# The first layer of a two-layer transformer kernel: from a looped order of phases to an unrolled pipeline of 20 slots a batch

## The reference

```python
# self attention: rows quantised to 8 bit, ternary weights, 16 heads of 16
q, k, v = bitlinear(x, w_q), bitlinear(x, w_k), bitlinear(x, w_v)
attn = softmax(causal(q @ k.T / sqrt(16)))
x = layernorm(x + bitlinear(attn @ v, w_o))
# cross attention: channels are the 128 rows, 16 heads of 8, 256 positions, rope, a mask
q, k, v = wq @ x + bq, wk @ ctx + bk, wv @ ctx + bv
scores = where(mask == 0, -1e4, rope(q).T @ rope(k) / sqrt(8))
x = layernorm(x + wo @ (softmax(scores) @ v) + bo)
```

## Time and profile before

| | us |
|---|---|
| median of 3 runs (lowest, highest) | 1825.73 (1823.53, 1825.94) |
| the profiled execution | 1822.41 |
| its span | 1820.6 |
| PE busy | 1453.8 (80%) |
| DVE busy | 999.8 (55%) |
| ACT busy | 609.2 (33%) |
| POOL busy | 366.7 (20%) |

### The profile page before, as it was taken

One profiled execution on the slowest core, in us unless ns is written; L12 is line 12 of the kernel. 1 busy time (PEld: TensorE's weight loads), 2 busy tenths in 40 slices (PEclk: granted clock), 3 DMA queues, 4 the chain that ended last, 5 costly groups with the idle time before them and its releaser, 6 DMA issues. The chain is left out here.

```text
span 1820.6 us, 29862 instructions
## 1 busy us (share of the span) xinstructions
PE 1453.8 (80%) x9331; PEld 863.5 (47%) x9331; DVE 999.8 (55%) x2735; ACT 609.2 (33%) x1389; POOL 366.7 (20%) x507
## 2 busy tenths in 40 slices
PE   2478888878888787539999996558888886799997
PEld 1234444444444443226566564335565553466664
DVE  5256666666666665242222222357887763467775
ACT  0133333334333332212232232225566543233231
POOL 1211112112111110011111111445555430000000
PEclk9589999999999998769999998678999998799999
DMA  4323222222223221054111111384455420200000
GB/s 127 104 47 51 47 45 50 48 48 50 53 52 53 47 40 22 29 193 133 36 35 31 34 33 36 76 186 98 115 116 120 104 64 19 74 1 12 12 1 24
DMA packets 165279, 112.22 MB, mean 62 GB/s; under 512 B 32682, under 2 KB 155818, under 8 KB 165040
## 3 DMA queue, kind: packets, MB, share of 16 engines
q1 hardware_dynamic: 150256, 95.09, 23.1%
q0 software_dynamic: 3408, 9.31, 2.0%
q10 hardware_dynamic: 11504, 6.46, 1.3%
HBM read 46.48 MB, written 12.45 MB: 32 GB/s over the span
## 5 line engine op out<-in xcount | busy, mean ns | idle before, releaser
L910 ACT ACTIVATE first_probs<-pair 128x512 f32<-128x512 f32 x320 | 177.6, 595 | 131.3 <-PE pair L411 129.0
L452 DVE TENSOR_REDUCE first_negmax_x<-bank 128x2 f32<-128x512 f32 x256 | 169.0, 685 | 64.0 <-PE bank L396 57.7
L396 PE MATMUL bank<-kept_stack_cross 96*128 96x256 bf16 x768 | 156.1, 286 | 11.4 <-DMA kept_stack_cross<-second_parts_x_q 9.5
L1891 ACT ACTIVATE second_probs<-pair 128x512 f32<-128x512 f32 x192 | 113.7, 598 | 130.7 <-PE pair L411 115.5
L411 PE MATMUL pair<-kept_stack_cross 98*128 98x256 bf16 x768 | 151.3, 280 | 1.5 <-DMA kept_stack_cross<-second_rows_x 1.0
L389 PE MATMUL bank<-kept_mask_q,kept_ident 128*128 128x512 bf16 x256 | 104.8, 409 | 57.4 <-DMA kept_stack_cross<-first_parts_x_q 31.6
L1405 PE MATMUL pair<-kept_w,experts_hidden_t 128*128 x312 | 140.3, 592 | 0.0
L452 DVE TENSOR_REDUCE second_negmax_x<-bank 128x2 f32<-128x512 f32 x128 | 88.6, 692 | 60.4 <-PE bank L396 52.5
L396 PEld LDWEIGHTS bank<-kept_stack_cross 96*128 96x128 bf16 x768 | 75.7, 103 | 75.5 <-issue 26.2
L404 PE MATMUL pair<-kept_mask_t,kept_ident 128*128 128x512 bf16 x256 | 100.8, 394 | 11.7 <-ACT first_probs L910 8.3
L1446 ACT ACTIVATE experts_hidden_t<-bank,kept_b 128x128 f32<-128x128 f32 x156 | 44.6, 368 | 183.2 <-PE bank L1380 183.2
(11 more groups left out here) (430 smaller groups left out, 2965.7 us busy)
## 6 DMA issues: line engine op xcount, KB each, us to landing
kept_stack_self<-first_parts_a SPq DMA_DIRECT2D x128, 64.0 KB, 3.1
kept_w<-in_L_ffn_W SPq DMA_DIRECT2D x8, 1024.0 KB, 7.1
kept_stack_self<-second_parts_a SPq DMA_DIRECT2D x128, 64.0 KB, 3.4
kept_stack_cross<-first_parts_x_k SPq DMA_DIRECT2D x96, 64.0 KB
kept_stack_cross<-first_parts_x_q SPq DMA_DIRECT2D x96, 64.0 KB
kept_stack_cross<-second_parts_x_k SPq DMA_DIRECT2D x96, 64.0 KB, 2.5
kept_stack_cross<-second_parts_x_q SPq DMA_DIRECT2D x96, 64.0 KB
expert_out<-experts_expert_done SPq DMA_DIRECT2D x39, 128.0 KB, 1.8
```

Of the source, the lines that this page charges most:

```text
L396: mm = pe.matmul(out, q, k, start=mask is None, stop=True, skip_group_check=True)
L452: return dve.tensor_reduce(negmax[:, 2 * n:2 * n + 2], bank[:, :].rearrange("p (m t) -> p m t", t=D), AX.X, ALU.max, negate=True)
L910: act.activation(probs[(phase + n) % PROBS][:, :], key_bank[n % KEYBANKS][:, :], ACT.Exp, scale=att.scale).then_inc(probs_made, 1)
L1891: act.activation(probs[i % PROBS][:, :], key_bank[i % 2][:, :], ACT.Exp, scale=att.scale).then_inc(probs_made, 1)
```

## The change

run_steps, Counts and step are gone. In their place stands the table of the second layer with 20 slots a batch: each step has an offset, and step f of batch b is done in slot 20 b + f. Each engine goes through all slots and does in each what falls in it, in a fixed order: first the slot's score bank and key bank. Own scores lie at 0 to 3, cross scores at 39 and 44 to 58, own keys at 9 to 12, cross keys at 65 to 68 and 73 to 84, so every slot of a full lap has one score bank and one key bank, of different batches: when batch b has its own scores, b-2 has its cross scores and b-3 or b-4 its cross keys. Buffers are added for it: three of x0, kv, the cross stack, four of x1, twelve probs tiles in place of eight. DVE has a drain at the end of each slot.

The small matmuls get other banks: `work` for what is made of rows and context, `small_bank` for turned maxima, sums, y and logits. The lay of the reciprocals is issued by ACT, no more by SP. DVE's own_heads has one reciprocal and one product over all heads, in place of two. The stack of the self attention is laid part by part. W1 gets its place after the first layer only, so load_expert now loads all three weights, 2 MB an expert; three experts (AHEAD) come in the routing stage, and in the experts' stage SP first waits until tile 0's rows are turned. The second layer uses the same classes; its instructions and their order stay.

```diff
+class Slots:
+    def batch_at(self, slot, offset):
+        b, rest = divmod(slot - offset, self.window)
+        return b if rest == 0 and 0 <= b < B else None
 ...
-        x0 = [sb(f"x0_{u}", [P, D]) for u in range(2)]
+        x0 = [sb(f"x0_{u}", [P, D]) for u in range(3)]
 ...
+        slots = Slots(20)
+        OWN_SCORES, CROSS_SCORES, OWN_KEYS, CROSS_KEYS = 0, ((39, 1), (44, 15)), 9, ((65, 4), (73, 12))
+        LOAD_ROWS, ROW_SCALES, ROUND_ROWS, TURN_ROWS, COPY_ROWS, MAKE_QK, SCALE_QK, MAKE_V, COPY_V, TURN_QK, COPY_QK = -33, -25, -24, -18, -18, -16, -16, -14, -13, -12, -12
+        SPLIT_SELF, STACK_FIRST, STACK_SECOND, STACK_THIRD = -8, -7, -6, -5
+        OWN_TWO, TURN_OWN_MAXIMA, OWN_ROWS, OWN_VALUES, COPY_OUT, TURN_OUT, OWN_HEADS, HEAD_SCALES, ROUND_HEADS = 3, 5, 5, 14, 15, 17, 18, 19, 20
+        TURN_HEADS, COPY_HEADS, MAKE_O, OWN_SUM, ROOT_A, OWN_END = 22, 22, 24, 25, 25, 27
+        LOAD_CONTEXT, MAKE_CROSS_K, ROTATE_K, SPLIT_KEYS, STACK_KEYS = 5, 11, 12, 15, 25
+        MAKE_CROSS_Q, ROTATE_Q, STACK_QUERIES = 29, 29, 31
+        MAKE_CROSS_V, COPY_CROSS_V, CROSS_TWO, TURN_CROSS_MAXIMA, CROSS_ROWS = 53, 53, 58, 60, 60
+        CROSS_VALUES = (70, 78, 82, 86)
+        COPY_CROSS_OUT, CROSS_RECIPS, LAY_RECIPS, SPREAD_SUMS, CROSS_HEADS, MAKE_Y, CROSS_SUM, ROOT_X, CROSS_END = 87, 89, 90, 92, 92, 94, 95, 96, 98
+        STORE_ROWS, TURN_X2, COPY_X2, MAKE_LOGITS, KEEP_LOGITS = 99, 101, 101, 103, 104
 ...
+            def cross_scores(b, n):
+                i = query_lane.index("cross", b, n)
+                if n == 0:
+                    pe.wait_ge(stack_q[b % 3], SIDE * (b // 3 + 1))
+                    pe.wait_ge(stack_k[b % 3], SIDE * (b // 3 + 1))
+                if i >= 2:
+                    pe.wait_ge(reduced, i - 1)
 ...
+            for s in SLOTS:
+                kind, b, n = query_lane.slot.get(s, (None, 0, 0))
+                if kind == "own":
+                    own_maximum(b, n)
+                if kind == "cross":
+                    cross_maximum(b, n)
 ...
+                dve.drain()
 ...
-    weights = (("L0_ffn_W2", "w2"), ("L0_ffn_W3", "w3"))
+    weights = (("L0_ffn_W1", "w1"), ("L0_ffn_W2", "w2"), ("L0_ffn_W3", "w3"))
 ...
-AHEAD, IOTAS = 4, 5
+AHEAD, IOTAS = 3, 5
 ...
+            sp.wait_ge(rows_turned, 1)
             for n in range(TILES):
```

More of the change, by code:

```diff
@@ L877, in _, with exponential @@
         @block.scalar
         def _(act):
-            for e in range(NE):
-                act.dma_start(t["w1"][:, e, :, :], d["L0_ffn_W1"][e].rearrange("(k p) f -> p k f", p=P)).then_inc(t["expert_loaded"][e], 16)
             act.preload_act_table(ACT.Exp)
+            def exponential(kind, b, n):
+                att, i = (SELF0 if kind == "own" else CROSS0), key_lane.index(kind, b, n)
+                if i % GROUP == 0 and i >= RING:
+                    act.wait_ge(probs_used, (i - RING) // GROUP + 1)
+                act.wait_ge(key_scored, i + 1)
+                act.activation(probs[i % RING][:, :], key_bank[i % 2][:, :], ACT.Exp, scale=att.scale).then_inc(probs_made, 1)
@@ L1021, in _ @@
-            run_steps(pool, first, step)
+            for s in SLOTS:
+                if (b := slots.batch_at(s, ROOT_A)) is not None:
+                    root(stats_a, var_a_made, rstd_a_made, b)
+                if (b := slots.batch_at(s, ROOT_X)) is not None:
+                    root(stats_x, var_x_made, rstd_x_made, b)
+                if (b := slots.batch_at(s, SPLIT_SELF)) is not None:
+                    split_self(b)
+                if (b := slots.batch_at(s, SPLIT_KEYS)) is not None:
+                    split_keys(b)
@@ L1141, in _ @@
-            run_steps(dve, first, step)
+                dve.tensor_tensor(t["logits"][:, b, :], small_bank[:, 0:NE], t["bg"][:, :], ALU.add).then_inc(logits_kept, 1)
+            for two in (two_a, two_x):
+                dve.memset(two[:, :], 0.0)
+            dve.drain()
+            for s in SLOTS:
+                kind, b, n = query_lane.slot.get(s, (None, 0, 0))
+                if kind == "own":
+                    own_maximum(b, n)
+                if kind == "cross":
+                    cross_maximum(b, n)
+                if (b := slots.batch_at(s, OWN_TWO)) is not None:
+                    own_two(b)
+                if (b := slots.batch_at(s, CROSS_TWO)) is not None:
+                    cross_two(b)
+                if (b := slots.batch_at(s, CROSS_RECIPS)) is not None:
+                    cross_recips(b)
+                if (b := slots.batch_at(s, CROSS_HEADS)) is not None:
+                    cross_heads(b)
+                if (b := slots.batch_at(s, CROSS_SUM)) is not None:
+                    cross_sum(b)
+                if (b := slots.batch_at(s, OWN_HEADS)) is not None:
+                    own_heads(b)
+                if (b := slots.batch_at(s, HEAD_SCALES)) is not None:
+                    head_scales(b)
+                if (b := slots.batch_at(s, ROUND_HEADS)) is not None:
+                    round_heads(b)
+                if (b := slots.batch_at(s, OWN_SUM)) is not None:
+                    own_sum(b)
+                if (b := slots.batch_at(s, OWN_END)) is not None:
+                    own_end(b)
+                if (b := slots.batch_at(s, CROSS_END)) is not None:
+                    cross_end(b)
+                if (b := slots.batch_at(s, KEEP_LOGITS)) is not None:
+                    keep_logits(b)
+                if (b := slots.batch_at(s, ROTATE_Q)) is not None:
+                    rotate(b, 0)
+                    split_queries(b)
+                if (b := slots.batch_at(s, ROTATE_K)) is not None:
+                    rotate(b, 1)
+                if (b := slots.batch_at(s, COPY_V)) is not None:
+                    copy_v(b)
+                if (b := slots.batch_at(s, ROW_SCALES)) is not None:
+                    row_scales_of(b)
+                if (b := slots.batch_at(s, ROUND_ROWS)) is not None:
+                    round_rows_of(b)
+                dve.drain()
@@ L1600, in second_layer_attentions @@
         block = ctx.enter_context(nc.Block())
+        slots = Slots(12)
         OWN_SCORES, CROSS_SCORES, OWN_KEYS, CROSS_KEYS = 0, ((32, 4), (40, 4)), 9, ((49, 8),)
```

936 lines of the change are left out of this document (445 added, 491 removed).

## The result

The changed kernel takes 1791.67 us (median of four runs, 1789.57 to 1794.1), the kernel before 1824.63 (four runs). The ratio is 0.9824, with an interval from 0.9801 to 0.9847: 33 us or 1.8% faster, where 75 had been forecast (1750, range 1716 to 1784). The direction was right, the size less than half. The profiled execution has a span of 1792.3 us against 1820.6.

What follows compares the result with a forecast made beforehand. PE and DVE were taken to wait for each other in the first layer. At 36.5 us a lap against 40.85, that stage saves 74, experts 1: 1822.4 becomes 1747.4, plus 3.3 to the median 1750.7, forecast 1750, range 1716 to 1784.

Steps and rivals of the forecast that it cites:

- What bounded it: First layer before the change: PE and DVE wait for each other, in one cross-score and one cross-key phase; batch 40.85 us.
- The rate of PE's work: First layer, one lap of 20 slots: PE's own work sums to 30.3 us, level with DVE's 30.2.
- The waits: First-layer lap: PE waits at slots 9, 18, 1 and 2 and inside slots raise 30.3 to 36.05 us.
- The contention: Slots 8 and 9: POOL's split_self slows DVE's split_queries on SBUF; 0.45 us a lap, bounds 0 and 2.2.
- Filling: First layer's start: slot 0 at 60 us, queries' product at 85, slot 40 at 102, slot 80 at 166.
- the 110 that I had named as a sign of being wrong: First layer's start: slot 40 coming after 110 us would show the forecast wrong; it was forecast at 102.
- Emptying: First layer's end: three laps of 29, 24 and 17 us, five slots, a 16 us tail; stage ends at 694.
- Experts: Routing and experts' stages: 4 us back at the first gather, 3 lost to late weights; together -1, bounds -4 and +8.
- Second layer: Second layer and last stage: instructions don't change, so 0 us.
- contention and SP's queue: First layer: POOL blocks all it can in slot 9, self stack late at slot 0; lap 38.5 to 39, 1777; chance 0.17.
- the two banks don't decouple: First-layer slots each cost the larger engine's part: lap 40.5, or 44.5 with hand-overs, total 1846; chance 0.05.
- the moved load that hurts: Experts' stage: each of experts 4 to 7 arrives 4 us late, +15, total 1765; chance 0.07.

Runs made afterwards that it cites:

- the version with all edits: Changed kernel plus POOL's split delayed, row scales and small DMAs a slot earlier, cross values' product later, expert weights one more ahead, fewer DVE drains: 1733.43 us, ratio 0.9512.
- the load change alone: Kernel before with only the experts' weights changed: W1 out of the first layer, three experts loaded in the routing stage: 1829.06 us, ratio 1.0049.
- the version with five edits: Changed kernel plus POOL's split delayed, row scales and small DMAs a slot earlier, cross values' product in slot 15, weights one more ahead: 1740.56 us, ratio 0.9544.
- the run with SP's waits: Changed kernel, SP laying the cross keys' stack only once the lap's own rows of maxima and copied sums have landed: 1790.34 us, ratio 0.984 to the kernel before.

## Why the prediction missed the size

**What bounded it** was right: PE's waits for the queries' stack and DVE's for the turned output went. DVE's own time was right too: from 150 to 600 us it waits 88 us, 7.5 of a lap of 38.2, and 30.7 are left, where 30.2 had been added up. The overlap with POOL is in it, 0.8 in eight laps of eleven, which the forecast counted beside the 30.2.

**The steps that failed.** No single one makes up the 46.7 us; the lap is the largest with 18.5. Its sum was 30.3 of PE's work and 6.2 of waits. In the seven laps at a clock of 1.00 PE is busy 31.4 and idle 6.8. So of the 1.7 us by which a lap is longer, 1.1 are PE's work, which the sum had too small, and 0.6 the waits, where the list was wrong.

**The rate of PE's work.** I had 30.3. A full-clock lap of the changed kernel has 31.23 busy with seven waits, one of the version with all edits 30.66 with three, for 276 matmuls each. A matmul ahead of a wait runs its 0.38 to the end, where one with a follower is overlapped by 0.16. So by these two laps a wait costs some 0.15 more than its idle time, about 1 us for the seven of a lap (an estimate); my sum had counted them at their idle time alone. The other part of the mean of 32.0 is the clock: a lap at 0.96 is busy up to 32.9. Four laps of eleven have it here, two in the kernel before. Such a lap in the middle is 0.6 longer (38.8 for 38.2), as part of the waits shrinks.

**The waits**, by place, a lap, forecast and measured: slot 18 2.0 and 1.66; slots 1 and 2 1.6 and 1.20; slot 13 1.0 and 0.67; slot 8 0.5 and 0.18; slot 9's rotation 0.4 and none; slot 12 0.25 and 1.08; the contention 0.45, which lies in the one at slot 12; and the rows of the own maxima none and 1.53. Their idle sum over all eleven laps, 6.4, is near the 6.2 forecast, but that is luck: the errors cancel. **The list of what slot 9 and slot 12 wait for is the wrong part.** I had "DVE has its maximum, the reciprocals and the rotation and split of the queries" and let PE wait 0.25 after it. I didn't ask when the DMAs of rows and sums land. In the kernel before neither stood in a line of the waits; here six stack transfers run ahead of them. The experiments show these two and the overlap with POOL to be one knot: undoing only the rows' wait gave next to nothing (lap 38.2 to 38.0, the sums then held DVE), undoing only the traffic gave the wait to the own stack and to slot 12, and undoing the overlap gave 0.8.

**The contention** was called: the operation took 1.23 for 0.43, and without the overlap 0.42. I had taken 0.45 for it between 0 and 2.2. It cost 0.8 in eight laps of eleven, 0.6 in the mean, and 0.8 a lap in the experiment. That DVE waits until POOL's whole operation is over is what the Trainium skill, SBUF — State Buffer, Who interferes with whom, states. But by that rule alone I had put all three waits and 2.2 us (a lap of 38.2; the 38.5 that I gave for the full contention is more than this sum), and only one of the five operations was caught. The one ahead of it on DVE began 0.01 before POOL's (425.19) and kept its 0.42, while POOL's took 1.43 in place of 1.16; the three behind it found POOL done.

**Filling.** Slot 40 came at 110.60 for 102, past the 110 that I had named as a sign of being wrong:

```profile
61.05 0.61 PE L386 MATMUL bank<-kept_causal_q,kept_ident 128*128 128x512 bf16 x1 [11.11 <-DMA kept_stack_self<-first_parts_a]
...
89.98 1.22 PE L782 MATMUL bank<-first_x,kept_xw_t 128*128 128x256 f32 x2
...
104.78 0.61 PE L386 MATMUL bank<-kept_mask_q,kept_ident 128*128 128x512 bf16 x1 [6.42 <-DMA kept_stack_cross<-first_parts_x_q]
...
110.60 0.61 PE L386 MATMUL bank<-kept_causal_q,kept_ident 128*128 128x512 bf16 x1 [4.79 <-DMA kept_stack_self<-first_parts_a]
```

The queries' product was forecast at 85 and came at 89.98. x1 is ready at 87.67, but the product has its place in slot 29, behind the scores and keys of batch 1; batch 1's own stack had held up slot 20 by 1.85 and the heads' rounding with it. The rest is SP and the transfers: issues to 105.73, and the last own part lands 4.9 later, not 3 to 4. From slot 40 to 80 the clock is low too, 0.77 from 100 to 160 us where it was 0.93 before: PE had been idle 6.42 and 4.79 in a row.

**Emptying.** 132.7 for 126.5 us. After slot 300 each short lap has the same chain of the sums' DMA, the reciprocals' DMA and y. The last logits:

```profile
729.28 0.17 DVE L1134 TENSOR_TENSOR kept_logits<-pair,kept_bg 128x8 f32<-128x8 f32 x1 [2.34 <-PE pair L831]
```

I have no experiment on this part, so its cause stays open; that it is the DMA chain is read from the trace alone (from 600 us on DVE waits 17.2 us for the sums and PE 7.3 for the laid reciprocals).

**Experts.** The first gather came back as forecast: from the last logits 31.8 us in place of 35.1, 3.4 for 4. PE waited 5.37 for it in place of 8.94. The weights were worse:

```profile
761.21 0.69 PE L1412 MATMUL bank<-kept_ident,experts_expert_rows 128*128 128x128 f32 x2 [5.37 <-DMA experts_expert_rows<-x_mid,kept_row_of]
...
793.92 1.55 PE L1436 MATMUL bank<-kept_w,experts_expert_rows_t 128*128 x3 [1.98 <-DMA kept_w<-in_L_ffn_W]
```

Tile 4 waited 1.98 and one more 2.5, and from the first gather on the stage is 7.1 longer than in the first profile of before (325.5 for 318.4). I had 3. The two tiles take 10.2 and 12.4 us, where all behind them take 8.0. The loads one more ahead take all of it away: 318.6. In the second profile of before the stage has 322.0, since the clock was 0.83 in its first 40 us and one tile took 9.8 for 6.7; against that profile routing and experts together are 1.2 shorter, the -1 of the forecast. So of the 4.6 us in the table a part is the clock of one execution. By its times the load change alone costs +5 to +13 us, where I had set -4 to +8, but the trace has no loss up to the experts' end. Subtracting one ratio from the other, the pipeline alone would be worth some 41 us; no run shows it by itself.

**Second layer.** I had 0 and found 6.7 with the last stage, 5.8 of it in the second layer. Its instructions are the same. The trace shows where it lies: in single laps with a lower granted clock. This is one of them behind one at full clock:

```profile
1287.13:1307.66 20.53, 17.42 (x174) 11.82 (x172) 16.55 (x42) 11.92 (x27) 11.36 (x16) 1.00 0.52 115
1307.66:1331.09 23.43, 20.42 (x191) 13.24 (x192) 17.49 (x41) 12.91 (x30) 11.24 (x16) 0.93 0.50 107
```

It is 3 us longer than the same lap of the kernel before (20.4 at 1.00), and a short lap near the end takes 17.28 at 0.80 for 15.65 at 0.94. The load change alone has a lap of 22.64 at 0.92 and one of 19.47 at 0.59, and the version with five edits has no full lap below 1.00 and 434.5 us. What sends the clock down in one execution and not in another stays open. The two profiles of the kernel before have no full lap below 1.00 in this layer either, and all but one of the kernels with the load change are longer there, by 3 to 9 us; whether that is chance isn't shown.

**The rivals.** The time lies nearest the one named contention and SP's queue (lap 38.5, 1777). Its lap was right within 0.3, and its contention came; but SP's queue made the own stack late by only 0.12 a lap, and what it delayed was the small DMAs on ACT's queue. That the two banks don't decouple is refuted by the lap of 38.2. Of the moved load that hurts, the two late weights came true, with 7 us in the experts' stage where it had put 15 on the total.

## What to carry to other kernels

When phases are dealt out over slots, write down for each slot not only what the engines do but when each DMA it needs was issued and what else is in the DMA engines then: two transfers of 4 KB behind six of 64 KB held PE for 1.5 us a lap, and no engine's busy time shows it. In an order of slots one misplaced step of 1.8 us cost 1.5 in every lap, so look first for the slot in which the slower engine idles. And waits that follow each other cover each other: a single one taken away may give nothing, and more of its worth is seen after the next is gone as well. Last, read the clock lap by lap before a difference of a few us is put down to the change.

## What the runs showed of the hardware

- Two DMAs of 4 KB, issued behind the first of six transfers of 64 KB on another queue, were there mostly 6.0 to 6.1 us after the first one's issue (416.53 to 422.65), and within 4.25 us with the key stack held back (the run with SP's waits). A DMA of the sums was used 3.5 to 3.9 us after its issue in the one and 1.95 in the other.
- Two engines on SBUF: DVE's 0.43 us operation took 1.23, until POOL's operation had ended, and 0.42 without the overlap. POOL's operation, which began 0.01 behind a DVE operation that kept its 0.42, took 1.43 for 1.16.
- PE's busy time for the same 276 matmuls at a clock of 1.00 is 31.23 us a lap with seven waits and 30.66 with three: busy time holds some of the waiting. At a clock of 0.96 it is 32.84.
- The granted clock differs from lap to lap and from execution to execution of a kernel: one lap of the second layer took 23.43 us at 0.93 in one profile of the changed kernel, and 20.39 at 1.00 in the other.
